# State space scan: which of the sixteen states get their inputs from VectorE and which from ScalarE and TensorE

## The reference, cut to what matters

```python
decay = jnp.exp(dt[..., None] * A)
inp = (dt * x)[..., None] * Bm[:, :, None, :]

def step(s, td):
    dec, ip, c = td
    s = dec * s + ip
    y = jnp.einsum('bdn,bn->bd', s, c)
    return (s, y)
s0 = jnp.zeros((B, D, N), h.dtype)
_, y = lax.scan(step, s0, (decay, inp, Cm))
y = y + D_skip * x
```

## Time and profile before

| what | value |
|---|---|
| median of 3 runs | 4070.98 us (4070.77 to 4076.35) |
| profiled execution, its own time | 4072.39 us |
| span of its trace | 4070.8 us |
| the phase `ssm_scan`, from its first scan to its last output | 273.1 to 986.7 us |
| VectorE busy in the stretch from 247 to 988 us | 673.67 of 741 us |
| TensorE, GpSimd, ScalarE busy in it | 653.29, 649.21, 595.23 us |

### The profile page before, as it was taken

The page is one execution under the profiler, slowest core; times in us unless marked ns, Lnnn a source line. Parts: engine busy times, 40 slices in busy tenths (PEclk is TensorE's granted clock), DMA queues, the critical chain, the costliest instruction groups (busy, mean ns, idle before and its releaser), DMA issues. The chain is left out here.

```text
span 4070.8 us, 64939 instructions
## 1 busy us (share of the span) xinstructions
PE 3424.0 (84%) x19567; PEld 2028.8 (50%) x19568; DVE 3169.5 (78%) x4175; ACT 2440.9 (60%) x4384; POOL 1304.4 (32%) x905
## 2 busy tenths in 40 slices
PE   8969899987559799797999999999999964289950
PEld 3445555544458688795333333333333333179950
DVE  8959999997866566477898898989989813368768
ACT  6768888886954433210588888888888841033323
POOL 4439899986014454201000000000000006644520
PEclk9979999998879899897899999999999985599975
DMA  6664444444869632494123232222322124222258
GB/s 216 247 217 165 161 159 157 161 165 155 270 181 256 182 105 78 113 291 117 28 54 73 53 73 55 58 71 52 75 53 60 24 78 124 72 80 92 90 169 291
DMA packets 531452, 521.10 MB, mean 128 GB/s; under 512 B 84784, under 2 KB 441264, under 8 KB 531040
## 3 DMA queue, kind: packets, MB, share of 16 engines
q1 hardware_dynamic: 517248, 480.45, 39.9%
q0 software_dynamic: 13952, 37.74, 2.7%
HBM read 301.15 MB, written 215.71 MB: 127 GB/s over the span
## 5 line engine op out<-in xcount | busy, mean ns | idle before, releaser
L2323 DVE TENSOR_REDUCE at_top<-at_psM 128x1 f32<-128x1024 f32 x1024 | 1206.2, 1220 | 135.9 <-PE at_psM L2174 135.1
L2283 ACT ACTIVATE at_probs<-at_psS 128x512 f32<-128x512 f32 x2048 | 1060.8, 604 | 250.4 <-PE at_psS L2200 250.4
L2200 PE MATMUL at_psS<-at_q,at_k 64*128 64x512 f32 x2048 | 794.9, 468 | 8.3 <-ACT at_probs L2283 8.3
L2174 PE MATMUL at_psM<-at_k,at_q 62*128 62x512 f32 x2048 | 689.3, 451 | 36.7 <-DMA at_vraw<-scratch_vf 21.9
L575 POOL TENSOR_TENSOR sc_prod<-sc_state,sc_c_row 128x1024 f32<-128x1024 f32 x256 | 648.7, 2564 | 84.4 <-DVE sc_state L726 73.5
L2174 PEld LDWEIGHTS at_psM<-at_k,at_q 62*128 62x128 f32 x2048 | 312.6, 190 | 601.4 <-DVE at_top L2323 519.4
L726 DVE TENSOR_TENSOR_SCAN sc_state<-sc_dec,sc_psI 128x1024 f32<-128x1024 f32 x256 | 574.2, 2276 | 43.5 <-PE sc_psI L647 32.9
L2213 PE MATMUL at_psV<-at_probs,at_v 128*32 128x512 f32 x4096 | 546.0, 605 | 0.0
L658 PE MATMUL sc_psY<-sc_prod,sc_ident 128*128 128x512 f32 x1024 | 479.2, 598 | 15.6 <-DVE sc_y L712 15.6
L2200 PEld LDWEIGHTS at_psS<-at_q,at_k 64*128 64x128 f32 x2048 | 337.2, 184 | 195.6 <-ACT at_probs L2283 191.3
L2141 POOL COPY at_v<-at_vraw 128x256 f32<-128x256 f32 x32 | 12.8, 401 | 1253.3 <-DMA at_vraw<-scratch_vf 1169.2
(11 more groups left out here) (393 smaller groups left out, 4936.0 us busy)
## 6 DMA issues: line engine op xcount, KB each, us to landing
sc_c_row<-scratch_bc SPq DMA_DIRECT2D x128, 512.0 KB, 3.7
scratch_xs<-at_zeros SPq DMA_DIRECT2D x140, 264.0 KB, 4.7
sc_b_row<-scratch_bc SPq DMA_DIRECT2D x32, 512.0 KB, 4.9
ec_y<-scratch_ys SPq DMA_DIRECT2D x32, 512.0 KB, 6.3
ex_x<-scratch_xs SPq DMA_DIRECT2D x39, 264.0 KB, 2.8
si_x<-in_x SPq DMA_DIRECT2D x16, 512.0 KB, 4.5
scratch_xn<-si_xn SPq DMA_DIRECT2D x16, 512.0 KB, 5.2
scratch_x_t<-si_xT SPq DMA_DIRECT2D x16, 512.0 KB, 5.8
```

Of the source, the lines that this page charges most:

```text
L2174: ins = pe.matmul(psM[t % 2][:, half * TILE:(half + 1) * TILE], rows_of(q4[j], h, 0, MAXROW)[:, c * P:(c + 1) * P], rows_of(k4[j], h, 0, M ...
L2200: pe.matmul(psS[v % 3][:], rows_of(k4[j], h, 0, GROUP)[:, c * P:(c + 1) * P], rows_of(q4[j], h, 0, GROUP)[:, half * TILE:(half + 1) * TILE ...
L2283: act.activation(probs[:, slot(j, v), :], psS[v % 3][:], ACT.Exp).then_inc(act_done, 1)
L2323: dve.tensor_reduce(top[j % 2][:, h, c:c + 1], psM[t % 2][:], AX.X, ALU.max, negate=True).then_inc(maxed, 1)
```

## The change

The list of states whose inputs VectorE makes shrinks from four (2, 6, 10, 14) to two (4, 10). The other two pairs' worth of units, four in a batch, are made by ScalarE and TensorE instead. The place at which the next batch's u is turned stays at unit 20, now the second state of the list.

```diff
@@ def ssm_scan(nc, A):
     CHUNKS = T // P
     ROWS = 4
-    MIXED = (2, 6, 10, 14)
+    MIXED = (4, 10)
     DIAG = tuple(n for n in range(S) if n not in MIXED)
...
         PER = S * H
-        TURN = MIXED[2] * H
+        TURN = MIXED[1] * H
```

## The result

The changed kernel takes 4063.76 us in the median of 15 runs (4059.95 to 4070.64), against 4070.98 us (4060.78 to 4076.35, 15 runs) for the one before on the same chip. The ratio is 0.998 with a 95% interval of 0.9973 to 0.9987: faster, by 7.2 us or 0.2%. Forecast were 17 us. The profiled execution took 4063.84 us, its span is 4062.2.

What follows compares the result with a forecast made beforehand. TensorE, at 2.593 us a unit, was taken to bound a run after four VectorE-paced units; terms of -12.4, -2.1, -1.9, -0.9, +0.75 and -0.4 sum to -17.0 us, giving 4054.0 us against the median 4070.98, range 4046 to 4064.

Steps and rivals of the forecast that it cites:

- what paces a run: Runs of units between mixed pairs: scans keep VectorE's 2.20 us for four units, then TensorE's transposes and adding, 2.593 each.
- the formula for a run: Run of L units: last scan starts 6.23 + (L - 3) x 2.593 us behind the scan before the run.
- rival 3: ScalarE paces the long runs: -9 us instead of -17.0, 4062 us; chance 5%.
- rival 1: VectorE is the bound after all, TensorE hides: 1.41 us saved for each of 32 units, -45, 4026 us; chance 3%.
- the outputs: Batch outputs y, behind scans 2 and 3: cost falls from 1.90 to 0.40 us a batch, by a walk.
- rival 2: Wait for the outputs moves into the run, 2.2 us in seven batches: -1.6, 4069 us; chance 6%.
- the swap: Removing mixed pairs saves 0.5 us each; with the outputs, -16.6 from scan 21 of batch 0 to the last output.
- step "the two mixed units after it take 3.63 and 3.60, together 7.23": Pair of units with VectorE-made inputs behind each run: scan, multiplication and register work take 7.23 us, TensorE idle in part.
- step "a scan starts 1.23 us behind its T": In TensorE-paced runs each scan follows its transposes (T) by 1.23 us; if not, in the long run, the forecast is wrong.
- the turning's 2.38: Turning of the next batch's u at units 19 and 20: costs 2.38 us a batch in both kernels.
- -0.4 for the start of batch 0: Up to scan 21 of batch 0, where ScalarE has no lead yet: 331.2 against 331.63 us, -0.4.
- Rival 4: TensorE's clock falls, now in a TensorE-paced run instead of under mixed units: slower; chance 5%.

Runs made afterwards that it cites:

- the two amended kernels: Kernel before (four pairs) and changed kernel with states 6 and 10, both with VectorE's loop written out and product 19 held: 4028.02 and 4010.69 us.
- The short product 6: Changed kernel with GpSimd's product of unit 6 covering 8 of the 1024 tokens in batches 1 to 7: 4062.22 us against 4071.0.
- the second set: One of three sets of experiment runs on three chips; the kernel before has a median of 4071.0 us in it.
- the first and third: The other two sets of experiment runs, each on its own chip; the kernel before has medians of 4039.61 and 4040.73 us in them.

## Why the prediction was wrong by half

**Right: what paces a run.** TensorE is continuous, scans follow it at 2.593 us, and the formula for a run holds. From scan 21 of batch 3 over 13 units it is right to the hundredth, 32.16 us, and redone for the two amended kernels, with two terms from the experiments, its sum gives their batches to 0.02 us. The adding's idle time of 0.1 us and the 51.4 us of the scans for `sc_psI` are what I had named as the mark of it. With half of the adding taken away a scan started every 2.19 us for ten units, until ScalarE was the bound, so the cause is shown. The scans waited 1.1 us in all for `sc_dec` in the stretch of the changed kernel, so rival 3 is out as well, and rival 1 by the size of the gain.

**Right: the outputs.** The wait of 2.20 us is gone, and the outputs cost about 0.3 us for each batch, not 1.90; rival 2 is out. The pair at (2, 10) brings back 5.2 us.

**Right in size, but in another kernel: the swap.** Its sum for the stretch was -16.6. Between the two kernels freed of the jump, of product 19 and of the pair's collision the swap measures 641.34 to 625.06, -16.3. That the two numbers are so near is in part luck: in written-out code a pair costs 0.32 us less, so taking one away is worth less, and at state 6 the outputs cost nothing instead of the walk's 0.40, which is worth more. What shows the terms right are the two batches above, 86.86 and 84.61. In the kernel as changed the stretch measures -10.05, and the difference is two new costs that the sum had at nothing.

**Wrong, step "the two mixed units after it take 3.63 and 3.60, together 7.23".** I carried this price from a pair that GpSimd has caught up with to one that follows the outputs and four fast scans, and I wrote that GpSimd "keeps up" and "does not pace a run". It does not pace it, but VectorE's multiplication has to wait for the end of its product: at 2.34 us a product against 2.20 a scan it falls behind in every fast stretch, and the pair now comes while product 6 is under way. From scan 7 to scan 9 it is 4.18 + 3.60 = 7.78 us and not 7.23; with 0.6 us in seven batches that is 4.2 us. The short product 6 shows it (the multiplication at its bare 1.21, and 4.2 of the 5.1 us gained), and the move to state 6 removes it.

**Wrong, step "a scan starts 1.23 us behind its T".** It holds where the loop does not jump. Where it does, scan 0 starts 3.50 us behind its T (531.74 and 535.24), behind 2.58 and 2.47 us of idle time at the two jumps, 2.8 us net for both. This is the sign that the prediction itself had named for being wrong. The prediction named the long run over the batch's end as the gain and did not ask what VectorE does between scan 31 and scan 0. In the kernel before that place lay among fast scans and cost 0.4 us at one jump and nothing at the other. Writing the loop out shows both: the late scan is gone from the changed kernel, and the kernel before gains little more than its register work.

**Wrong, though it cancelled: the turning's 2.38.** It was the same in both kernels, so the sum did not suffer, but 1.1 us of the 2.38 was the wait for product 19 and not the turning; holding that product gave 6.1 us. The prediction's -0.4 for the start of batch 0 measured -0.8, but the start differs by more than that between two traces of one kernel, so this term was not tested.

**Rival 4** was nearly absent: one adding of 3.41 us in the trace, at a granted clock of 0.55, which cost 0.7 us, and the kernel before had three such places in its stretch. The granted clock of the whole execution, 0.92, is that of before.

**Open: the last 2 us.** Behind the scan the changed kernel takes 2.3 us more. The kernels of the second set, whose code behind the scan is the same, have 3086.1, 3088.1, 3088.6 and 3093.5 us there, and those of the first and third 3051.9 to 3059.3. This spread is larger than the difference. Whether the change has a part in it was not settled.

## What to carry to other kernels

A price that is read from one place of a pipeline holds only with its surroundings: before carrying it to another place, ask for each engine whether it is caught up there, here GpSimd above all, beside whose products VectorE's multiplication took 1.81 and 2.33 us instead of 1.21. Ask too whether instructions stand ready for an engine at its loop's jump: where five scans did, the jump cost 0.4 us and nothing, and where each scan had to wait for its transposes 1.4 us each time, of an idle time of 2.58 and 2.47. The change turned a fast stretch into a paced one and so laid the jump bare. When a sum misses by half, mend both kernels of the suspected costs and measure the change again: here that told a wrong mechanism from a right one with two omissions.

## What the runs showed of the hardware

VectorE's jump to the start of its loop left it idle for 2.47 and 2.58 us where nothing covered it, and cost 0.4 us and nothing at the two places where five scans stood ready. Instruction transfers stand beside it in the traces: within 0.5 us behind the last scan ahead of the bare jump (532.67 us) two of 8 KB start, VectorE's next scan starts at 535.24 behind 2.58 us of idle time, and where the loop is written out one of the two and the late scan are gone. In the kernel before a transfer starts 2 us ahead of the end of that scan (535.3 and 537.42 us), and the jump costs 0.4 us. That VectorE waits for such a transfer is my inference from these times. By their shares of the 16 DMA engines a transfer takes 0.35 us there (8.7% of 0.5 us for two) and 0.48 with the loop written out (6.0% for one), so most of the 2.58 us is not the transfer itself, and no run shows what fills them.

Writing VectorE's loop out was worth 8.1 us of 655.0 in the kernel before: the register work in front of instructions (0.19 us behind each multiplication, 0.1 in five scans) is small, but it stands on the path some eight times in a batch.

A VectorE multiplication of 128x1024 took 1.21 us alone, 1.81 or 2.33 with a product of GpSimd ahead of it; a product took 2.37 alone and 3.25 with a multiplication ahead.
